# Pacing GpSimd's indirect DMAs in four stages of a one-core transformer tower

## The reference, cut to what matters

```python
# attention of the third pair: 64 sequences, 8 heads of 64 channels, plain softmax
scores = einsum('bshc,bthc->bsth', q, k) * SCALE
u = einsum('bsth,bthc->bshc', softmax(scores, axis=2), val)

# feed-forward of the third pair: 262144 random edges between the 16384 tokens give the gates
e = leaky_relu(a_src[src] + a_dst[dst])
ee = exp(e - segment_max(e, dst)[dst])
alpha = ee / (segment_sum(ee, dst)[dst] + 1e-16)
agg = segment_sum(h[src] * alpha[:, :, None], dst)       # h: 4 heads x 4 values of a token
# ... agg decides top-2 of 4 experts, and those are applied

# feed-forward of the fourth pair: top-2 of 16 experts, hidden width 128
hidden = silu(x @ w1) * (x @ w2)
out = sum_e dispatch[:, :, e] * (hidden_e @ w3_e)
```

## Time and profile before

| | us |
|---|---|
| Median of 3 runs | 7117.53 (7095.68 to 7121.69) |
| The profiled execution, its own time | 7065.35 |
| Its span, first to last instruction | 7063.6 |
| PE (TensorE matmul) busy | 5207.5, 74% |
| DVE (VectorE) busy | 4857.2, 69% |
| ACT (ScalarE) busy | 2513.5, 36% |
| POOL (GpSimd) busy | 2356.7, 33% |
| Mean granted clock of TensorE | 0.858 |

### The profile page before, as it was taken

The page is one execution under the profiler, slowest core; times in us unless marked ns, Lnnn a source line. Parts: engine busy times, 40 slices in busy tenths (PEclk is TensorE's granted clock), DMA queues, the critical chain, the costliest instruction groups (busy, mean ns, idle before and its releaser), DMA issues. The chain is left out here.

```text
span 7063.6 us, 110641 instructions
## 1 busy us (share of the span) xinstructions
PE 5207.5 (74%) x40671; PEld 3476.1 (49%) x40671; DVE 4857.2 (69%) x8912; ACT 2513.5 (36%) x4368; POOL 2356.7 (33%) x2332
## 2 busy tenths in 40 slices
PE   4659878865256999970899999999950889429928
PEld 3542255543134666650677777777740268403602
DVE  7869988887534888860678788787762577617417
ACT  3534433333223666640233333333320432103302
POOL 0010010013577000007666666666636010160550
PEclk8879989976577999985899999999975989659959
DMA  0200001113210000000111111111110000200510
GB/s 16 73 5 1 24 24 35 35 39 107 33 15 16 2 2 2 2 33 12 34 38 38 38 43 38 38 38 38 38 26 8 1 3 3 60 24 1 143 22 17
DMA packets 248039, 205.02 MB, mean 29 GB/s; under 512 B 118154, under 2 KB 222515, under 8 KB 245843
## 3 DMA queue, kind: packets, MB, share of 16 engines
q1 hardware_dynamic: 178174, 145.16, 7.2%
q0 software_dynamic: 69456, 54.00, 5.1%
q10 hardware_dynamic: 12, 0.39, 0.0%
HBM read 112.11 MB, written 67.84 MB: 25 GB/s over the span
## 5 line engine op out<-in xcount | busy, mean ns | idle before, releaser
L3370 PE MATMUL edges_bank<-part_room,hot_room 128*128 128x512 f32 x7168 | 1709.3, 399 | 340.4 <-DVE hot_room L3461 189.4
L3370 PEld LDWEIGHTS edges_bank<-part_room,hot_room 128*128 128x128 f32 x7168 | 1365.5, 192 | 684.2 <-issue 228.0
L3352 POOL DMA_INDIRECT XT<-gat_node_table,edges_idx x1152 | 1200.1, 1042 | 643.8 <-issue 307.2
L3391 ACT COPY XT<-edges_bank 128x512 f32<-128x512 f32 x896 | 502.5, 603 | 1162.8 <-PE edges_bank L3370 851.0
L3479 DVE COPY_PREDICATED XT<-edges_tabs_p,XT 128x1024 f32<-128x1024 int32 (+3 forms) x896 | 632.0, 705 | 43.2 <-DVE edges_acc_s L3527 7.3
L3461 DVE TENSOR_SCALAR hot_room<-edges_lanes,edges_nodes 128x512 fp32r<-128x512 f16 x896 | 384.6, 492 | 340.5 <-PE edges_bank L3370 224.2
L1792 ACT ACTIVATE GT<-attc_sct 128x1024 f32<-128x1024 f32 x256 | 262.1, 1024 | 492.9 <-PE attc_sct L1712 311.5
L1778 ACT ACTIVATE GT<-attc_sc,attc_nm 128x256 f32<-128x256 f32 x1024 | 399.6, 480 | 79.6 <-issue 58.5
L1843 DVE TENSOR_REDUCE attc_mx<-attc_sc 128x4 f32<-128x1024 f32 x256 | 313.3, 1224 | 166.2 <-PE attc_sc L1701 99.4
L1701 PE MATMUL attc_sc<-XT,attc_tT 64*128 64x256 f32 x2048 | 308.8, 422 | 118.8 <-ACT GT L1778 79.5
L505 POOL TENSOR_TENSOR X<-H,ln_f_mean 128x1024 f32<-128x1024 f32 x5 | 11.4, 2279 | 916.3 <-DVE ln_f_shift L542 916.3
(11 more groups left out here) (836 smaller groups left out, 10288.3 us busy)
## 6 DMA issues: line engine op xcount, KB each, us to landing
edges_lanes<-gat_places SPq DMA_DIRECT2D x224, 128.0 KB
gat_states<-GT SPq DMA_DIRECT2D x32, 768.0 KB
XT<-gat_node_table,edges_idx POOLq DMA_INDIRECT x1152
expert_pairs<-in_L_ffn_W_dram SPq DMA_DIRECT2D x48, 256.0 KB
XT<-XT SPq DMA_DIRECT2D x32, 256.0 KB
XT<-XT SPq DMA_DIRECT2D x64, 128.0 KB
XT<-XT SPq DMA_DIRECT2D x128, 64.0 KB
sorted_in<-stats SPq DMA_DIRECT2D x1, 5056.0 KB
```

The costliest lines, as they stand in the source:

```text
L3352: nc.gpsimd.indirect_dma_start(out=rows[:, k, c, :], out_offset=None, in_=q.t_table, in_offset=bass.IndirectOffsetOnAxis(ap=idx[:, k, c:c ...
L3370: m = nc.tensor.matmul(banks[t % BANKS][:], hot[:, (k * GROUPS + j) % 2, b, t, :], parts[:, p, b].rearrange("p u c -> p (u c)"), start=b = ...
L3391: nc.scalar.copy(fetched[:, (k * GROUPS + j) % 2, t].rearrange("p u c -> p (u c)"), banks[t % BANKS][:]).then_inc(fetched_in, 1)
```

## The change

The waits on TensorE's `bank_full` in the edge stage's `gather` go. In their place GpSimd clears a small buffer of 128x64 numbers before each fetch; each clearing waits for the one before. The loop now covers all chunks, the first two as well. In the three other stages the indirect DMAs, which ran without waits, get waits behind the steps of the stage: in the search, DMA n of 256 (but not the first) waits for 15n/16 steps of scores; in scatter and fetch, DMA n of 128 waits for (n-8)/2 finished units, where that is over zero.

```diff
@@ -749,6 +749,7 @@
 
 
 SORTED, SLOTS_TILE, COLLECT = TILES // 2, 2 * P, 8
+AHEAD_OF_UNITS = 8
 
 
 class GateSplit:
@@ -872,18 +873,20 @@
     def clear(self):
         self.nc.gpsimd.memset(self.zeros, 0.0).then_inc(self.blank, 1)
 
-    def scatter(self, pool):
+    def scatter(self, pool, beat):
         pool.wait_ge(self.cleared, 16)
         for t in range(SORTED):
             for c in range(2):
+                beat(2 * t + c)
                 self.nc.gpsimd.indirect_dma_start(
                     out=self.rows_in, out_offset=bass.IndirectOffsetOnAxis(ap=self.slot[:, t, c:c + 1], axis=0),
                     in_=self.g.X[:, TILES - SORTED + t, :], in_offset=None).then_inc(self.scattered, 16)
 
-    def fetch(self, pool):
+    def fetch(self, pool, beat):
         back = self.g.X[:].rearrange("p (t c) d -> p t c d", c=2)
         for t in range(SORTED):
             for c in range(2):
+                beat(2 * t + c)
                 self.nc.gpsimd.indirect_dma_start(
                     out=back[:, t, c, :], out_offset=None, in_=self.rows_out,
                     in_offset=bass.IndirectOffsetOnAxis(ap=self.slot[:, t, c:c + 1], axis=0)).then_inc(self.fetched[t // 8], 16)
@@ -1236,10 +1239,15 @@
 
             @block.gpsimd
             def _(pool):
+                def beat(n):
+                    units = (n - AHEAD_OF_UNITS) * NU // (2 * SORTED)
+                    if units > 0:
+                        pool.wait_ge(hid_full, units)
+
                 if spread is not None:
-                    spread.scatter(pool)
+                    spread.scatter(pool, beat)
                 if collect is not None:
-                    collect.fetch(pool)
+                    collect.fetch(pool, beat)
 
             @block.tensor
             def _(pe):
@@ -1641,7 +1649,12 @@
                 pool.wait_ge(pool_made, 2)
                 nc.gpsimd.tensor_copy(pair_sum[D:P, :], g.ident[D:P, D:P]).then_inc(pool_made, 1)
                 pool.wait_ge(pool_made, 3)
-                g.order.search(pool)
+
+                def beat(n):
+                    if n:
+                        pool.wait_ge(s_full, -(-n * 15 // 16))
+
+                g.order.search(pool, beat)
 
             @block.tensor
             def _(pe):
@@ -2824,7 +2837,7 @@
     def spare(self):
         return self.bufs[1 - self.parity_at]
 
-    def search(self, pool):
+    def search(self, pool, beat):
 
         gp, g = self.nc.gpsimd, self.g
         C = 16
@@ -2844,6 +2857,7 @@
 
             def fetch(n):
                 for c in range(n * C, (n + 1) * C):
+                    beat(turn * TILES + c)
                     gp.indirect_dma_start(out=rooms[n % 2][:, c - n * C, :], out_offset=None, in_=table,
                                           in_offset=bass.IndirectOffsetOnAxis(ap=self.index[:, c:c + 1], axis=0)
                                           ).then_inc(self.gathered[n % 2], 16)
@@ -3058,7 +3072,7 @@
 LOW_PLACES = TILES // BLOCKS
 LOW_BITS = LOW_PLACES.bit_length() - 1
 HOT_COLUMNS = CHUNKS * ON_PE
-PACE_BEHIND = 3 * PER_GROUP
+SPACER = 64
 
 
 class HotPlaces:
@@ -3263,6 +3277,7 @@
         inp_s, acc_s, decay = (st.sb(n, [P, HEADS2, 1 + PERH, W]) for n in ("inp_s", "acc_s", "decay"))
         lanes = st.sb("lanes", [P, GROUPS, PER_GROUP, P], F16)
         att = st.sb("att", [P, CH])
+        spacer = st.sb("spacer", [P, SPACER])
         nodes_i, nodes = st.sb("nodes_i", [P, BLOCKS], I32), st.sb("nodes", [P, BLOCKS])
         pow2 = st.sb("pow2", [P, LOW_BITS], I32)
         tabs_p, weights_p, dst_p = (st.ps(n, [P, 512]) for n in ("tabs_p", "weights_p", "dst_p"))
@@ -3290,6 +3305,7 @@
         (split, numbered, powers, att_in, hot_ready, bank_full, fetched_in, halved, selected, pe_passed, act_passed, dve_passed, bits_ready) = (
             st.sem(n) for n in ("split", "numbered", "powers", "att_in", "hot_ready", "bank_full", "fetched_in", "halved", "selected",
                                 "pe_passed", "act_passed", "dve_passed", "bits_ready"))
+        spaced = st.sem("spaced")
         cleared, own, idx_ready, rows_used, passed, diff_ready, exped, sums_ready, state_ready, starts_used = (
             st.sem(n) for n in ("cleared", "vec_own", "idx_ready", "rows_used", "pool_passed", "diff_ready", "exped",
                                 "sums_ready", "state_ready", "starts_used"))
@@ -3343,21 +3359,21 @@
                 for s in range(LOW_BITS):
                     nc.gpsimd.memset(pow2[:, s:s + 1], LOW >> (s + 1)).then_inc(powers, 1)
 
-                def gather(n, k, banks_before):
+                pool.sem_inc(spaced, 1)
+
+                def gather(n, k):
                     pool.wait_ge(idx_ready, n + 1)
                     wait_apart(pool, rows_used, n + 1, passed)
                     for c in range(BY_DMA):
-                        if c:
-                            wait_apart(pool, bank_full, banks_before + c * ON_PE // BY_DMA, passed)
+                        wait_apart(pool, spaced, n * BY_DMA + c + 1, passed)
+                        nc.gpsimd.memset(spacer[:], 0.0).then_inc(spaced, 1)
                         nc.gpsimd.indirect_dma_start(
                             out=rows[:, k, c, :], out_offset=None, in_=q.t_table,
                             in_offset=bass.IndirectOffsetOnAxis(ap=idx[:, k, c:c + 1], axis=0)).then_inc(gathered[k], 16)
 
-                gather(0, 0, 1)
-                gather(1, 1, ON_PE - 4)
-                with pool.Fori(1, NI) as i:
+                with pool.Fori(0, NI) as i:
                     for k in range(2):
-                        gather(2 * i + k, k, (2 * i + k) * ON_PE - PACE_BEHIND)
+                        gather(2 * i + k, k)
 
             @block.tensor
             def _(pe):
```

## The result

| | before | after |
|---|---|---|
| Median of 4 runs, us | 7106.60 (7094.55 to 7121.69) | 7427.16 (7419.01 to 7439.18) |
| Ratio, with its 95% interval | | 1.045 (1.042 to 1.048) |
| Span of the profiled execution | 7063.6 | 7428.9 |
| Mean granted clock of TensorE | 0.858 | 0.837 |

The forecast was 6510 us; the kernel became 4.5% slower. In the changed kernel L1792 is L1805, L1373 is L1381, L3527 is L3543, L3352 is L3370, L3391 is L3407, and the clearing is L3369. These are the source lines of after (count, shortest/median/longest in ns, first and last start); they answer to the earlier trace rows.

What follows compares the result with a forecast made beforehand. It took TensorE's semaphore signals, held while GpSimd issues indirect DMAs too fast, to bound the kernel. 7065.35 - 232 - 143 - 146 - 52 = 6492, plus a third of the median's 52 us: 6510 us, range 6410 to 6760.

Steps and rivals of the forecast that it cites:

- the price of the clearing: Edge stage: each clearing adds 0.171 + 0.07 = 0.24 us, so a fetch comes every 1.58 us, undisturbed 1.49.
- The rest of that sum: Edge stage: 57 us a chunk, GpSimd the bound, last scan at 5189 instead of 5241, 52 us saved.
- rival 1: Edge stage: the clearing hides in the gap, signals stay held, 82 us a chunk, 7350 us in all; chance 0.07.
- The search: Attention stage: waits put the search's DMAs 3.57 us apart, no signal is held, 232 us saved in three terms.
- (a): Attention stage, before the first scores: prompt signals let L1843 start at 1866 instead of 1897.0, 31 us saved.
- (b): Attention stage, first L1843 to first L1792: eight steps of scores take 22 us instead of 44, 22 us saved.
- (c): Attention stage, the 38 steps up to 2265: 145 us instead of 324, at 3.81 us a step, 179 us saved.
- Scatter and collection: Expert stages: two DMAs a unit, expd 205 us instead of 348.1 (143 saved), expe 218 instead of 363.8 (146 saved).
- The threshold: All these stages: TensorE's signals are held while indirect DMAs come faster than one in 1.43 us.
- Rival 3: All changed stages: the loss goes with each DMA, not with their crowding; 7060 to 7120 us; chance 0.06.
- Rival 4: Whole kernel: only the shared port matters, waits change nothing, clearings add 9 us, 7130 us in all; chance 0.04.
- Rivals 2 and 5: Edge stage: clearing dear, 1.81 us a fetch, 6780 us, chance 0.08; expert stages: still stall half, 6655 us, chance 0.07.

Runs made afterwards that it cites:

- e3: The changed kernel with an edge-stage clearing of 128x320 instead of 128x64: 6570.7 us, ratio 0.931 to before.
- e2: The changed kernel with an edge-stage clearing of 128x256 instead of 128x64: 6495.3 us, ratio 0.921 to before.
- e13: The changed kernel with 256 columns in the edge stage and, elsewhere, sixteen small clearings before each DMA instead of waits on steps: 6467.9 us, ratio 0.917.
- e7: The changed kernel with 256 columns in the edge stage and, elsewhere, four small clearings before each DMA instead of waits on steps: 7006.5 us, ratio 0.986.
- e9: The changed kernel with 256 columns in the edge stage and, elsewhere, eight small clearings before each DMA instead of waits on steps: 6835.2 us, ratio 0.964.
- e4: The changed kernel with two edge-stage clearings of 256 columns before each fetch, each behind the one before: 7278.2 us, one run.
- e14: e12 with a clearing of 128x192 before each edge-stage fetch as well: 6529.6 us, ratio 0.925 to before.
- e12: The changed kernel with the edge stage's old bank waits back, no clearing, and PACE_BEHIND 0 instead of 12: 6494.6 us, ratio 0.917 to before.
- e18: The edge stage of e12 with the search, scatter and collection of e13: 6471.9 us, ratio 0.913 to before.

## Why the prediction was wrong

**The step that failed** is the price of the clearing: "I take 0.171 + 0.07 = 0.24, because the next operation behind a fetch does start that early and the 0.30 belong to the fetch." Measured alone: 1.27 against 1.25, so 0.02. The row had it: if an operation can start 0.07 us after a fetch, then the 0.30 us in which the next fetch is made ready don't occupy GpSimd, and a short operation fits inside them. I read the row as the length of a further gap, not as a hole in the one I had counted. Every clearing showed this: 0.165, 0.273, 0.330 and 0.385 us (medians for 64, 192, 256 and 320 columns) and always 0.16 us behind it, so the distance is 0.94 + length + 0.16 (measured 1.27, 1.38, 1.44 and 1.50), and only what goes beyond 0.30 - 0.16 = 0.14 us is added. My estimate of 1.49 was what 320 columns give. So the mechanism of the forecast, that held signals vanish above a certain distance, was right; the distance that the clearing of 64 columns would give was not.

**The rest of that sum** followed from it. A fetch every 1.58 us, 57 us a chunk and GpSimd as the bound is what e3 shows, and e2 towards the end of its stage (1.616 and 1.557 us, 57.1 and 54.9 a chunk): right for a clearing four or five times as long. In after the fetches of a chunk came 1.45 us apart in the mean, (5816.7 - 3147.9 - 1004.3)/1151, but 1.27 where VectorE did not interfere, and signals were held. In place of -52 us the stage brought +794 and +60.

**The range.** I had the bounds 1.25 and 1.72 on paper and the threshold 1.43 between them, and still took 1.49 for the low end, where the time falls. Below the threshold the time doesn't fall but rises steeply: with (1.43 - 1.25)/(1.72 - 1.25) = 0.38 of the width on the bad side, a chance of 0.07 for rival 1 was far too small, and a range that ended at 6760 left out what one row could decide.

**Rival 1** is what happened: forecast 82 us a chunk, measured 82.9; forecast 7350, measured 7427. Its mechanism (a chunk's fetches let few banks through, the rest follow) is the one of the timeline, and its terms came as well: 10 banks in 49 us and 18 in 33 were forecast, and in chunks 4 to 30 ScalarE copied 9.4 banks in the 51 us of the fetches and 18.6 in the 33 us behind them. So this was not luck. It missed the later first scan, 60 us. Its "against" (1.49 for a fetch alone) was the failed step again.

**The search**: -232 forecast, -212 measured. (a) The first L1843, now L1856, comes 38 us earlier, 6 of them from earlier stages, so 32 for 31. (b) Then 31 us to the first L1792 instead of 44: 13 for 22. (c) From there to the last step 993.8 us instead of 1154.2: 160 for 179, since a step takes 993.8/255 = 3.90 us, not 3.81, with DMAs and additions beside it. (The 10.5 us a step that I gave for before takes in the 75 us up to the first step; term (c) doesn't.) **Scatter and collection**: -138 for -143 and -140 for -146; a unit takes 210.4/63 = 3.34 and 223.6/63 = 3.55 us, where 3.13 and 3.33 were forecast. The two DMAs of a unit follow each other at once, 1.26 us apart, and then comes a pause, 1.88 us from start to start. These steps are right, and e13 shows that they are right for the reason given.

**The threshold** of 1.43 us, from the run of ten fetches, was right as a place but wrong in kind: signals are held less and less from 1.25 to about 1.5 us, not fully below and not at all above. It also is a matter of runs: pairs at 1.26 us with 1.88 between them hold nothing (after, 6900 to 6950: 16 units in 50 us, as many as without DMAs), ten in a row at 1.25 do.

**Rival 3** (the loss goes with each DMA): the same 128 DMAs cost 138 us, then 84 (e7: 293.9 us), 28 (e9: 238.9) and nothing (e13: 199.9) against the 210.4 of after, by their distance alone. Its number falls with it. **Rival 4** (only the port): the Trainium skill, "SBUF — State Buffer", section "Who interferes with whom", has TensorE and ScalarE never wait. The traces agree for their instructions' lengths (L1792 and L1805, median 1023 ns in both kernels) and disagree for the signals: 19.9 us for a bank. By that rule e2, with a clearing twice as long as that of after (426.9 against 205.2 us in all), would be slower; it is 12% faster (0.921/1.045), although VectorE's one-hot operations did get longer, 594 ns against 489. **Rivals 2 and 5**: the clearing wasn't dear (but e4 shows a price of that kind, 80 us a chunk at 2.23 us), and the waits do pace.

Not settled: what it is behind GpSimd that holds TensorE's signals, and what differs between the chips. No run here takes that apart. That TensorE's signals are the ones held, and not those to TensorE, is read from the timelines; no run tests other engines' signals by themselves.

## What to carry to other kernels

Where engines stand idle beside a run of indirect DMAs from GpSimd, look at how late TensorE's results are used, and spread the DMAs, by waits or by filler work: 1.50 us in the edge stage (e3) and 1.70 in the expert stages (e13) were enough here, and 1.48 in the latter was not (e9); where a threshold lies inside the bounds of an unknown cost, the forecast has two outcomes and the chance goes by where the threshold stands. By the lengths measured, filler work of up to about 0.14 us between two indirect DMAs is free (an estimate; the shortest single clearing tried took 0.165 us and cost 0.02), and so it spaces nothing: measure the distance, not the filler. Long filler on GpSimd costs VectorE something too (e14). Prefer a pacing that corrects itself (e12, e18) to one that must meet a distance, since the distance that suffices differs from chip to chip.

## What the runs showed of the hardware

- TensorE's signals are used up to 20 us late while GpSimd issues indirect DMAs 1.21 to 1.27 us apart, up to 11 us at 1.38, up to 3.8 or 6.7 us at 1.44 by the chip, and not late at 1.50 and above (longest wait 2.4 us).
- ScalarE's signals to TensorE are prompt in the same stretches: 0.05 and 0.06 us in after at 4210 and 4192.
- Pairs of indirect DMAs 1.26 us apart, 3.14 us from pair to pair, hold nothing in the expert stage: 16 units in 50 us in after.
- Clearings on GpSimd lengthen VectorE's one-hot operations: 489 ns in the mean in after, 563 in e14 (192 columns), 594 in e2 (256), 617 in e3 (320).
- It goes by the number of DMAs: with 64 rows instead of 128 a fetch takes 0.90 us instead of 0.94, and the hold is the same (longest wait 20.5 and 19.8 us, one run each).
- A clearing of 128x64 between two indirect DMAs costs 0.02 us, though it takes 0.165; sixteen of 128x3 take 0.57 us (e13):

```profile
5899.94 0.57 POOL L1248 MEMSET expd_blank_room<- 128x3 f32 x16
```

- TensorE's granted clock falls with the waits: 0.81 over 3500 to 4500 us in after, where TensorE was busy 674 of the 1000 us, and 0.98 before, where it was busy 926 (the line is after; PE and PEld, DVE, ACT, POOL busy; clock; DMA share; GB/s):

```profile
3500.00:4500.00 1000.00, 674.28 (x2618) 534.40 (x2619) 533.17 (x1054) 257.38 (x406) 495.65 (x841) 0.81 0.12 25
```

- The same code takes 55 us a chunk on two chips and 59 on three, where the kernel before differs by only 0.4 to 0.6%.
